# A decoder layer for 64 sequences on one core: another order of all engines, without VectorE's one-element copies

## The reference

```
x = x + self_attention(layernorm(x))        # rope, causal mask, softmax, Wo, biases
x = x + cross_attention(layernorm(x), ctx)  # 77 keys, softmax, Wo, biases
h = layernorm(x)
logits = h @ router_w; p = softmax(logits); e = argmax; top = p[e]
routed = (h @ up_w[e] * silu(h @ gate_w[e])) @ down_w[e]      # e < 7, else none
shared = (h @ shared_up * silu(h @ shared_gate)) @ shared_down
x = x + 2 * top * routed + shared
```

## Time and profile before

| | us |
|---|---|
| median of 3 runs | 1080.29 (1079.55 to 1080.8) |
| the profiled execution | 1076.56 |
| its span, first to last instruction | 1074.7 |
| TensorE busy | 987.1 (92%) |
| VectorE busy | 870.5 (81%) |
| ScalarE busy | 738.3 (69%) |
| GpSimd busy | 631.6 (59%) |

### The profile page before, as it was taken

How to read it: one execution, slowest core, us unless ns; L and a number is a source line. 1 busy time by engine, 2 the same in 40 slices (tenths; PEclk the granted TensorE clock), 3 DMA queues, 4 the chain that set the end, 5 groups by cost and what they waited for, 6 DMA issues and landing times.

```text
span 1074.7 us, 45099 instructions
## 1 busy us (share of the span) xinstructions
PE 987.1 (92%) x16200; PEld 819.5 (76%) x16201; DVE 870.5 (81%) x2853; ACT 738.3 (69%) x1557; POOL 631.6 (59%) x1488
## 2 busy tenths in 40 slices
PE   1578999999999999999999999999999889999995
PEld 1356777777777777777777777777777889999995
DVE  3367999989999999989999999999996557777774
ACT  0266887888888787888878888887875245555552
POOL 0345667776767767676677767677664224444443
PEclk9999999999999999999999999999999999999998
DMA  5222111000010000000000000100010122222220
GB/s 132 70 71 71 33 29 32 28 28 27 25 32 26 30 25 28 29 25 30 25 29 28 25 30 25 31 26 30 26 28 24 60 66 71 72 68 71 67 67 5
DMA packets 66648, 44.27 MB, mean 41 GB/s; under 512 B 24135, under 2 KB 61451, under 8 KB 66592
## 3 DMA queue, kind: packets, MB, share of 16 engines
q1 hardware_dynamic: 55424, 30.35, 10.5%
q0 software_dynamic: 5312, 12.18, 3.3%
q10 hardware_dynamic: 5856, 0.99, 0.5%
HBM read 23.96 MB, written 18.29 MB: 39 GB/s over the span
## 4 chain that ended last, share of the span: by engine, by line
PE 62%; SPq 16%; DMA 6%; DVE 6%; issue 5%; ACT 2%; ACTq 1%; POOL 1%; DVEq 0%; POOLq 0%
SPq L391 12%; PE pv L1120 9%; PE scores L1300 6%; PE scores L1305 6%; PE ro L1316 6%; DMA arena<-arena 5%; PE scores L999 5%; PE ro L1175 4%; PE scores L1161 3%; PE ro L1137 3%; PE st L1230 3%; DVE arena L641 3%; PE scores L1167 2%; PE ro L1148 2%; PE pj L1143 2%
## 5 line engine op out<-in xcount | busy, mean ns | idle before, releaser
L641 DVE TENSOR_REDUCE arena<-scores 128x8 f16<-128x1024 f32 (+1 forms) x256 | 256.6, 1002 | 61.3 <-PE scores L1007 50.9
L919 ACT ACTIVATE arena<-scores 128x1024 f32<-128x1024 f32 (+1 forms) x256 | 262.6, 1026 | 57.7 <-PE scores L1016 44.6
L859 ACT ACTIVATE arena<-st 128x128 f16<-128x128 f16 (+2 forms) x256 | 155.0, 606 | 6.4 <-PE st L1230 5.4
L859 ACT ACTIVATE arena<-arena 128x512 f16<-128x512 f32 (+2 forms) x192 | 92.9, 484 | 71.4 <-POOL arena L453 51.4
L1120 PE MATMUL pv<-arena 128*32 128x128 f32 (+1 forms) x4096 | 139.1, 277 | 0.1
L1120 PEld LDWEIGHTS pv<-arena 128*32 128x32 f32 (+1 forms) x4096 | 104.6, 110 | 17.2 <-issue 10.1
L439 POOL TENSOR_TENSOR arena<-arena,neg_half 128x1 f32<-128x1 f32 x192 | 106.5, 555 | 15.0
L449 POOL TENSOR_TENSOR arena<-arena 128x256 f32<-128x256 f32 x64 | 46.5, 726 | 81.5 <-DVE arena L633 81.5
L526 POOL DMA_INDIRECT out_dram<-x_tile x70 | 69.9, 998 | 38.6 <-POOL carried L525 26.1
L477 POOL TENSOR_TENSOR arena<-arena 128x128 f32<-128x128 f32 x128 | 51.8, 404 | 60.2 <-DVE arena L651 60.2
L814 DVE SCALAR_TENSOR_TENSOR half_hid<-tanh_s,scores 128x512 f32<-128x512 f32 x70 | 48.1, 688 | 40.7 <-ACT tanh_s L964 40.6
(11 more groups left out here) (175 smaller groups left out, 2696.5 us busy)
## 6 DMA issues: line engine op xcount, KB each, us to landing
x_tile<-xs SPq DMA_DIRECT2D x70, 129.0 KB, 2.1
arena<-arena SPq DMA_DIRECT2D x512, 4.0 KB
arena<-in_x_dram SPq DMA_DIRECT2D x64, 64.0 KB, 1.8
out_dram<-pay SPq DMA_DIRECT2D x64, 64.0 KB, 1.6
arena<-in_ctx_dram SPq DMA_DIRECT2D x64, 38.5 KB
w_gate<-in_L_ffn_gate_w_dram SPq DMA_DIRECT2D x7, 256.0 KB, 2.6
w_up<-in_L_ffn_up_w_dram SPq DMA_DIRECT2D x7, 256.0 KB, 3.0
w_down<-in_L_ffn_down_w_dram SPq DMA_DIRECT2D x7, 256.0 KB, 4.1
```

Of the source, the lines that this page charges most:

```text
L641: v.tensor_reduce(nmax[:, n, :].rearrange("p (m r s) -> p r m s", r=2, s=SLOT)[:, u, :, 0:HG], pair(s)[:, :, 0:HG * keys].rearrange("p m ( ...
L859: return a.activation(to, of, ACT.Copy)
L919: a.activation(e32[0:rows, 2 * n + u, :], scores[0:rows, 1024 * s:1024 * (s + 1)], ACT.Exp).then_inc(sexp_done[n][u], 1)
```

## The change

`LAG` becomes 13. Every engine's `step` is written in another order, with other lags. On TensorE, once the lags are compared by sequence, the cycle is the same but for three things: `nmT_of 1` (the turned cross maxima) comes ahead of `xT_of 1`, not behind `project_q2`; `project_out 1` comes ahead of `shared_up`; and within three of the four pairs the two score turns swap places. The step also begins at another point of the cycle. The other engines move more. The core of the diff, without the rest of the tables:

```diff
-LAG = 11
+LAG = 13
@@ SyncE, step
+                at(i, p, 9, rows_of_max, 1)
+                at(i, p, 6, load_ctx)
+                at(i, p, 13, base_out)
                 at(i, p, 3, load_x)
                 at(i, p, 6, rows_of_max, 0)
-                at(i, p, 8, rows_of_max, 1)
-                at(i, p, 11, base_out)
-                at(i, p, 5, load_ctx)
@@ GpSimd
                 wait(pool, rot_ready, b + 1)
+                wait(pool, xb_ready[0], b + 1)
...
-                if n == 0:
-                    wait(pool, x_in_s[p], 8 * b + 16 - 8 * p)
                 g.tensor_tensor(resid[:, b, :], (x_in, x1)[n][:, p, :], out_bias[:, n, :], ALU.add).then_inc(xb_ready[n], 1)
@@ GpSimd, scatter
+                wait(pool, gate_ready, b + 1)
                 wait(pool, sh_added, b + 1)
+                wait(pool, token_ready, b + 1)
@@ VectorE
-            def carry(n):
-
-                v.tensor_copy(carried[:, n:n + 1], eps[:, :])
...
                 else:
-                    wait(dve, resid_done[1], b + 1)
                     rows = resid[:, b, :]
-                if n == 2:
-                    carry(3)
+                if n == 0:
+                    wait(dve, ln_mv[n], b)
                 v.bn_stats(bn6[:, n, :], rows).then_inc(ln_stats[n], 1)

+            def stats_seen(b, p, n):
+
+                wait(dve, ln_stats[n], b + 1)
+
+            def resid_seen(b, p):
+
+                wait(dve, resid_done[1], b + 1)
+
             def ln_mean_var(b, p, n):

-                wait(dve, ln_stats[n], b + 1)
-                carry(n)
                 v.bn_aggr(mv[:, n, p, :], bn6[:, n, :]).then_inc(ln_mv[n], 1)
@@ VectorE, the end of the new step
+                at(i, p, 3, stats_seen, 0)
+                at(i, p, 10, add_shared)
+                at(i, p, 3, ln_mean_var, 0)
+                at(i, p, 7, row_max, 1, 1, 0)
+                at(i, p, 6, add_attention)
@@ ScalarE, xn3_out
                 wait(act, ln3_shift, b + 1)
+                wait(act, scattered[place(b, p)], sent(b, p))
@@ TensorE
             def ready_cross_max(b, p):
-                pass
+                wait(pe, qkT2_ready, b + 1)
@@ TensorE, nmT_of
-                wait(pe, smax_done[n][0], b + 1)
                 wait(pe, smax_done[n][1], b + 1)
@@ TensorE, spare matmuls in early steps
-                early(i, 8, busy_scores, 0, ...)
+                early(i, 11, busy_scores, 0, ...)
```

More of the change, by code:

```diff
@@ new lines, in step @@
+                at(i, p, 7, ln_mean_var, 1)
+                at(i, p, 7, k2_bias)
+                at(i, p, 5, row_max, 0, 1, 1)
+                at(i, p, 9, turned, 1)
+                at(i, p, 7, q2_bias)
+                at(i, p, 9, recip, 1)
+                at(i, p, 5, row_max, 0, 0, 0)
+                at(i, p, 4, rope_products)
+                at(i, p, 10, logits_copy)
+                at(i, p, 9, turned_back, 1)
+                at(i, p, 10, top_of)
+                at(i, p, 10, marks_of)
@@ new lines, in step @@
+                at(i, p, 10, mark_top_of)
+                at(i, p, 9, add_cross)
+                at(i, p, 10, hot_of)
+                at(i, p, 9, resid_seen)
+                at(i, p, 10, half_of, 0)
+                at(i, p, 9, ln_stats_of, 2)
+                at(i, p, 9, stats_seen, 2)
+                at(i, p, 10, hidden_of, 0)
+                at(i, p, 9, ln_mean_var, 2)
+                at(i, p, 6, turned, 0)
+                at(i, p, 10, run_of)
+                at(i, p, 10, hot_pos_of)
@@ L1286, in _ @@
+                at(i, p, 9, values, 1)
+                at(i, p, 7, project_q2)
             run(pe, step)
```

169 lines of the change are left out of this document (71 added, 98 removed).

## The result

The changed kernel took 1082.44 us (median of 16 runs, 1080.85 to 1086.88) against 1078.58 for the one before (16 runs): ratio 1.0038, 95% interval [1.0025, 1.005]. It is slower by 0.4%. The forecast was 1066; the measured time lies inside the stated range of 1050 to 1084, but on the other side of no change.

What follows compares the result with a forecast made beforehand. SyncE's late transfers of maxima were taken to hold the 12.14 us step; GpSimd's loop would bind at 11.85. 50 x 0.29 gives -14.5, projections -2.0, ends +2.5: -14.0 from 1080.29, forecast 1066 us, range 1050 to 1084.

Steps and rivals of the forecast that it cites:

- The waits an operation ahead: VectorE's waits on statistics and residual, put one operation earlier: change which instruction holds the queue, not result times; counted as nothing.
- The copies: VectorE's four one-element copies a step, removed: 0.49 us a step in durations, but overlapped or beside idle time; counted as nothing.
- The loop over GpSimd: Turns, shared sum, GpSimd's norms and scatter, q2's bias, back to turns: 11.98 us, less 0.13 for overlaps, period 11.85.
- The way back: From q2's bias (0.31) over ScalarE's high part (0.42), GpSimd's low part (0.42), TensorE's turns to shared sum (6.60 us).
- SyncE's earlier start: Cross maxima turned and copied earlier: SyncE starts 3.1 us sooner, its 0.77 lateness and the 0.36 us DMA wait go.
- The fourth rival: Layer norm 2's power behind GpSimd's scatter delays q2's bias and stalls TensorE: 12.4 us a step, 1094 us; chance 0.11.
- The ends: Pipeline fill and drain: early spare matmuls delay the first transpose, +2.5 us (bounds -1 and +4.1); expert end nothing.
- The tail: Fewer spare matmuls before the expert tiles, where TensorE waited 1.02 us for the first transfer: nothing (bounds 0 and +1).
- the swapped projections in the drain: Cross output projection ahead of shared up projection, second residual ready earlier: 0.4 us for five steps, -2.0 (bounds 0, -2.9).

Runs made afterwards that it cites:

- The fastest version on B: Changed kernel with layer norm 1's mean and variance near k2's bias, layer norm 3's statistics behind hidden, 38 spare matmuls, early ones from step 5: 1080.86 us, 0.9689.

## Why the prediction was wrong

The period was forecast at 11.85 and measured at 12.23, 0.38 a step more. Two steps of the prediction failed, one for 0.15 of it and one for 0.23.

**The waits an operation ahead: "nothing for either" is the step that turned the sign.** With the copies it cost 7.9 us, 0.15 a step; without it the change stands at 0.9965. "They change which instruction holds the queue, not when the result is there" is true of the results. It leaves out that a wait is work of the queue, and that an instruction with three of them starts later behind the last: 0.40 and 0.20 us behind the product, against 0.24 and 0.13. The price of the waits by themselves, without the copies, is argued and not shown.

**The copies: no gain when they went.** They overlapped their neighbours, as the earlier trace rows showed. They also carried the waits. The Trainium skill ("VectorE: DVE Perf Modes", section "Rules for kernel authors") advises to minimise the number of operations, not of semaphores; here the trace disagrees: 2853 VectorE instructions with copies, 2597 without, and the longer list, with its waits in other places, is 7.9 us faster.

**The loop over GpSimd: there, but longer than the forecast, and with another way back.** With the copies and waits back it takes 12.08, 0.10 more than the sum of whole durations, 11.98; the other 0.13 are what the forecast took off for overlaps, and the row it names for them is of a copy that is not in the sum. From the shared add to q2's bias the rows gave 10.55 - 6.60 = 3.95 and two hand-overs, 4.06; it took 4.15 there, and 4.09 in the changed kernel. The way back was put through ScalarE's high part, GpSimd's low part and TensorE's turns of q2 and k2, 7.92 us. Between 300 and 700 us no turn waited for the low part. With the copies back it is TensorE's own work from the transpose that waits for q2's bias (7.9 us in 34 waits), 4.89 + 3.04 = 7.93: that the two sizes agree is luck. In the changed kernel it is VectorE's unbroken run to the hidden, 4.96, and 3.19 from there over the PSUM strip and the cross pair: 8.15.

**SyncE's earlier start: the mechanism right, the next bound wrong.** The DMA wait went whole and the transfers follow the copy at once. Alone it brought 12 us, of which 4.8 lie in 45 steps of the loop. The period fell by 0.11 of the 0.29 that the forecast counted. "It binds before TensorE alone would" is wrong for the order of before: there TensorE, with 81% of the chain, binds at 12.03. In the new order 11.95 was reached.

**The fourth rival** came out in sign only: the period rose by 0.09, not 0.26, and q2's bias waits for GpSimd just 0.16 us in every other step (2.7 us in 17 of 33 steps). Its mechanism is there, its price is not what made the kernel slower.

**The ends.** The first transpose came at 27.26 us, 3.6 later (23.69), inside the bounds. Two groups stand ahead of it:

```profile
23.68 2.08 PE L1193 MATMUL scores<-w_qkv 128*128 128x128 f32 x8 [0.78 <-DVE out_bias L601]
25.55 1.91 PE L1198 MATMUL ro<-w_qkv 128*128 128x128 f32 x8
27.26 0.42 PE L1144 MATMUL pj<-id,arena 128*128 128x128 f32 x1
```

At the first shared add 0.33 was left of it. The tail cost 1.1, just over its bound of 1: TensorE waited 3.87 us for the first tile instead of the 1.02 of the earlier trace rows, and the granted clock was 0.50 from 870 to 876 us, not only from 866 to 869. The prediction had fewer spare matmuls there and no lower clock. The 2.0 us of the swapped projections in the drain did not show; the ten last steps took 0.4 more.

## What to carry to other kernels

Where waits are moved off short operations, count how many land on each instruction that stands on the path: here the third one went with 0.07 to 0.16 us from the late event to the add. Before a loop's end is priced, follow each engine's unbroken run beside it, since what can be had ends where that run binds: 0.11 here, not 0.29. When a change bundles one good move with several "free" ones, try the good one alone: here it was 1.1% faster by itself and 0.4% slower in company. And try it on the kind of chip that counts: on B it gained nothing by itself.

## What the runs showed of the hardware that was not expected

**Two kinds of chip, and a scatter that stops TensorE.** On B the unaltered changed kernel's values matmuls break in the middle:

```profile
420.20 0.74 PE L1127 MATMUL pv<-arena 77*32 77x128 f32 x16
421.24 0.67 PE L1127 MATMUL pv<-arena 77*32 77x128 f32 x16 [0.31 <-issue]
```

```profile
419.96 1.08 POOL L496 DMA_INDIRECT xs<-pay,put  x1 [0.17 <-issue]
```

```profile
421.36 1.22 DVE L643 TENSOR_REDUCE arena<-scores 128x8 f16<-128x1024 f32 x1 [1.00 <-PE scores L1014]
```

TensorE goes on 0.20 us behind the end of GpSimd's indirect DMA (419.96 + 1.08 = 421.04), and VectorE hears of the self pair, done near 420.3, only at 421.36. In the nine traces on B in which the values matmuls start in the first half of the scatter, TensorE breaks off in each of the 274 steps between 300 and 700 us, and goes on 0.15 to 0.25 us behind the scatter's end. On A the changed kernel and the one with the copies back overlap the two in the same way, 33 times each, without a break of 0.1 us:

```profile
412.07 1.08 POOL L496 DMA_INDIRECT xs<-pay,put  x1 [0.16 <-issue]
```

```profile
412.32 1.08 PE L1127 MATMUL pv<-arena 77*32 77x128 f32 x32
```

In the variant with layer norm 1 moved, the scatter runs on B from 413.73 to 414.82, ahead of the values at 414.88 (in other steps it meets them for 0.07 us at most), and they take 1.08; that kernel's period there is 12.30 against 13.11. The changed kernel's first leg is 4.93 on B and 4.09 on A, its other two are within 0.04. The fastest version on B, in which the scatter meets only the first 0.2 us of the values, stands between: they take 1.31 us, and its first leg is 4.35, against 4.04 in the same steps on A. The coincidence is shown; that the scatter is the cause is argued from it, and no run on B moved the scatter alone. What makes a chip one kind or the other is open.

**A loop body can be too long.** With four steps in an iteration one step in each of the 12 rounds took 17.0 to 18.8 us instead of some 13.1, and between 300 and 700 us TensorE stood still for 3.4 to 3.8 us in each round, with no engine named that it waited for. Its instruction queue in the profile's list of queues (packets, MB, share):

```profile
q8 instruction: 142, 2.33, 0.9%
```

against the changed kernel's

```profile
q8 instruction: 40, 0.66, 0.3%
```

The 102 packets more are 8.5 for each of the 12 rounds. That fits a longer body that is loaded again in each round, and a body of two steps that is not, in 24; the cause was not tested further.
